# Two cross attentions on one core: their second halves with the chunk of heads as the outer loop and the block of keys as the inner one

## What is computed

```python
# layer 0: q and k are normalised per head; only keys with padding_mask count
attn = jnp.einsum('bihd,bjhd->bhij', q, k)
attn = jnp.where(padding_mask[:, None, None, :], attn, -jnp.inf)
ctx = jnp.einsum('bhij,bjhd->bihd', jax.nn.softmax(attn, axis=-1), v)
# layer 1: a mask per query and key
scores = jnp.einsum('bhqd,bhkd->bhqk', Q, K) / jnp.sqrt(jnp.float32(D))
scores = jnp.where(mask == 1, jnp.float32(-1000000000.0), scores)
out = jnp.einsum('bhqk,bhkd->bhqd', jax.nn.softmax(scores, axis=-1), V)
```

## Time and profile before

| | |
|---|---|
| median of 3 runs | 1674.43 us |
| lowest, highest | 1670.66, 1679.79 us |
| the profiled execution | 1673.19 us |
| its span in the trace | 1671.4 us |
| mean granted TensorE clock | 0.974 |
| L0x, second half | about 263 to 431 us |
| L1x, second half | about 1135 to 1321 us |

### The profile page before, as it was taken

One profiled execution on the slowest core, in us unless ns is written; L12 is line 12 of the kernel. 1 busy time (PEld: TensorE's weight loads), 2 busy tenths in 40 slices (PEclk: granted clock), 3 DMA queues, 4 the chain that ended last, 5 costly groups with the idle time before them and its releaser, 6 DMA issues. The chain is left out here.

```text
span 1671.4 us, 27782 instructions
## 1 busy us (share of the span) xinstructions
PE 1574.9 (94%) x9252; PEld 752.7 (45%) x9263; DVE 1025.3 (61%) x1708; ACT 523.2 (31%) x781; POOL 170.0 (10%) x126
## 2 busy tenths in 40 slices
PE   7999999999899889999999999998999899989997
PEld 3233332222333377666774433332222244477775
DVE  6778897999656541111112799998889746652223
ACT  3534555778213310000101111116567413200000
POOL 0522021000002010000002222102000001020002
PEclk9999998999999989999999999998999999989999
DMA  4433433220076667767762332113221021249996
GB/s 170 157 121 131 163 138 103 59 52 25 2 154 124 226 244 246 252 240 261 253 215 70 115 126 99 65 38 133 63 75 38 1 88 33 102 162 322 330 332 223
DMA packets 74460, 240.28 MB, mean 144 GB/s; under 512 B 7600, under 2 KB 21824, under 8 KB 55072
## 3 DMA queue, kind: packets, MB, share of 16 engines
q1 hardware_dynamic: 64752, 220.42, 39.6%
q10 hardware_dynamic: 7088, 10.69, 1.8%
q0 software_dynamic: 2560, 8.39, 1.5%
HBM read 214.04 MB, written 35.91 MB: 150 GB/s over the span
## 5 line engine op out<-in xcount | busy, mean ns | idle before, releaser
L1607 ACT ACTIVATE BIG<-banks 128x1024 f32<-128x1024 f32 (+5 forms) x320 | 282.2, 934 | 121.1 <-PE banks L1553 120.4
L1128 DVE CUSTOM_DVE_ANT_0 BIG<-banks,MASK,MX 128x512 bf16<-128x512 f32 (+5 forms) x384 | 229.1, 655 | 67.1 <-issue 38.7
L2173 PE MATMUL banks<-KF,BIG 128*128 128x160 f32 (+1 forms) x1792 | 229.0, 289 | 1.9 <-DVE KF L1870 1.9
L2173 PEld LDWEIGHTS banks<-KF,BIG 128*128 128x128 f32 x1792 | 226.9, 191 | 8.8 <-issue 8.8
L711 PE MATMUL banks<-KF,XN 32*128 32x512 f32 (+4 forms) x1280 | 188.4, 607 | 11.2 <-DVE MX L1128 3.3
L2143 PE MATMUL banks<-BIG,PB 128*128 128x512 f32 x448 | 198.0, 595 | 0.0
L1546 PE MATMUL banks<-XN,KF 32*128 32x512 f32 (+4 forms) x1280 | 187.8, 613 | 7.5 <-ACT BIG L1607 5.2
L1658 DVE TENSOR_TENSOR PB<-PB,BIG 128x2048 f32<-128x2048 f32 (+5 forms) x78 | 165.7, 2124 | 21.6 <-ACT BIG L1607 19.2
L1119 DVE TENSOR_REDUCE MXW<-banks 128x2 f32<-128x1024 f32 x128 | 149.4, 1216 | 29.0 <-PE banks L711 28.9
L1513 PE MATMUL banks<-BIG,V 128*32 128x512 f32 (+4 forms) x1280 | 159.8, 568 | 4.5 <-ACT BIG L1607 2.4
L2143 PEld LDWEIGHTS banks<-BIG,PB 128*128 128x128 f32 x448 | 82.9, 190 | 100.6 <-issue 100.5
(11 more groups left out here) (298 smaller groups left out, 1482.4 us busy)
## 6 DMA issues: line engine op xcount, KB each, us to landing
BIG<-in_L0f_w SPq DMA_DIRECT2D x64, 1024.0 KB, 4.8
BIG<-in_L1f_w SPq DMA_DIRECT2D x48, 1024.0 KB, 5.7
BIG<-in_mask_q SPq DMA_DIRECT2D x16, 1024.0 KB, 9.0
k_saved<-KF SPq DMA_DIRECT2D x32, 256.0 KB, 2.7
CT<-in_ctx SPq DMA_DIRECT2D x6, 1024.0 KB, 4.8
XNT<-in_ctx SPq DMA_DIRECT2D x6, 1024.0 KB, 5.6
v_saved<-V SPq DMA_DIRECT2D x24, 256.0 KB, 2.4
KF<-k_saved SPq DMA_DIRECT2D x24, 256.0 KB, 3.4
```

Source lines behind the costliest of these rows:

```text
L1128: last = v.tensor_tensor_reduce(m.JUNK[:, 2 * half + e, k0:k1], pair[:, e, k0:k1], bias, 1.0, mx, ALU.add, ALU.max, mx)
L1607: a.activation(m.PE_[:, s % NP, 2 * half:2 * half + 2, q0:q1], m.pair[(2 * s + half) % 3][:, :, q0:q1], ACT.Exp).then_inc(exp_ready, 1)
L2173: last = t.matmul(out, W1[k][:, d, f * P:(f + 1) * P], XE[:, d, :], start=d == 0, stop=d == DC - 1)
```

## The change

`weighted_by_chunk` takes the place of `weighted_values` in the two cross attentions (the self attentions keep the latter, without its dynamic parts). It loops over chunks outside and blocks inside. A **unit** is one chunk with one block, 4 steps. The first unit of a chunk uses the block in SBUF; the others (`others`) load a unit's keys, values and mask into a ring of 3 slots (KRING, VRING, and MBK or ROWRING). A chunk's products with V stay in one PSUM bank over all blocks and are copied out once (`copy_out`). The PSUM pairs begin anew with each chunk. Masks are made once, in the first half, saved with the keys and loaded with them: L1x has a new load, four new GpSimd instructions and a store of 512 KB per block there (`turned_mask`, `keep_mask`); L0x has one new VectorE instruction and a store of 128 KB (KEYROW). The clearing of PSUMS and OACC goes. The value for masked scores, NEG, is now -2^100.

```diff
+RING = 3
 # first half, sync
+            def keep_mask(j):
+                if L.row_mask:
+                    wait_alone(sp, masks_made, j * KT_ + KT_ + B)
+                    sp.dma_start(m.MSAVE[one(j)].rearrange("a p k n -> (a p) k n"), m.MBK[RING]).then_inc(mask_stored, 16)
+                else:
+                    wait_alone(sp, bias_ready, j + 1 + B)
+                    sp.dma_start(m.ROWSAVE[one(j)].rearrange("a p n -> (a p) n"), m.KEYROW).then_inc(mask_stored, 16)
...
 # first half, gpsimd
-            for c in range(DC):
-                g.memset(m.PSUMS[c], 0.0).then_inc(zeroed, 1)
-            g.memset(m.OACC[:, :, :], 0.0).then_inc(zeroed, 1)
...
+            def turned_mask(j):
+                pool.wait_ge(masks_loaded, j * 16 + 16 + B)
+                wait_alone(pool, mask_stored, j * 16 + 16 + B)
+                for kb in range(KT_):
+                    g.tensor_scalar(m.MBK[RING][:, kb, :], m.MK[:, kb, :], 1.0, m.RN[:, 0:1], ALU.is_equal, ALU.mult).then_inc(masks_made, 1)
...
 # first half, vector
+                v.tensor_scalar(m.KEYROW, m.KM[:, 0:KB], m.mask_factor, m.mask_offset, ALU.mult, ALU.add).then_inc(keys_counted, 1)
...
 # second half
+    GROUPS = -(-(NB - 1) // RING)
...
+    def others(eng, nb, c, body):
+        with eng.Fori(0, GROUPS) as group:
+            for r in range(RING):
+                with eng.If(group * RING + (r + 1) < nb):
+                    body(Unit(nb, c, group, r))
...
+            def load(u):
+                at, c, r = u.group * RING + u.r, u.c, u.r
+                wait_alone(sp, product_done, u.step(-KT_) + BP)
+                block = bass.ds(at, 1)
+                sp.dma_start(m.KRING[:, r, :], m.KSAVE[block, :, c, :].rearrange("a p n -> (a p) n")).then_inc(keys_loaded[r], 16)
...
+            for c in range(DC):
+                others(sp, nb, c, load)
+                if c == 0:
+                    O.load_output_weights(sp)
...
+            def unit(u):
+                flag = flag_of(u)
+                for k in range(1, KT_):
+                    scores(u, k, flag)
+                    times_values(u, k - 1)
...
+                with pe.If(at + 1 < nb):
+                    scores(follower, 0, flag_of(follower))
+                if u.c + 1 < DC:
+                    with pe.If(at + 1 >= nb):
+                        next_chunk(u.c)
+                times_values(u, KT_ - 1)
...
+            for c in range(DC):
+                unit(Unit(nb, c))
+                others(pe, nb, c, unit)
...
+            def copy_out(c):
+                dve.wait_ge(product_done, nb * (KT_ * c + KT_) + BP)
+                v.tensor_copy(m.OACC[:, c, :], m.bank[6 + c % 2]).then_inc(chunk_done, 1)
```

More of the change, by code:

```diff
@@ L1437, in weighted_values, with tile_free @@
     kt = L.order
[L1438 to L1446 removed]
+    m.fresh = []
+    O = project_out(nc, m, L, next_loaded, None)
+    def tile_free(s):
+        return max(0, s - NP + 1)
     class Parts:
@@ L1526, in scores @@
                     M.ready(pe, 1)
[L1527 to L1528 removed]
                 ks = slice(kt[k] * P, (kt[k] + 1) * P)
[L1530 to L1533 removed]
+                parts = BIAS_PARTS[L.fixed] if kt[k] in (0, KT_ - 1) else 1
                 def out(g):
@@ L1543, in scores @@
                 for g in range(G):
-                    if not biases and g % 2 == 0:
-                        pe.wait_ge(exp_ready, i * (2 * NS) + max(0, 2 * s - 2 + g // 2) + B)
-                    t.matmul(out(g), m.KF[rows(g), c, ks], m.QF[rows(g), c, q0:q1], start=not biases, stop=False)
-                if L.row_mask:
-                    with pe.If(flag > 0):
-                        for g in range(G):
-                            t.matmul(out(g), m.IDB[:, :], m.MBK[:, kt[k], q0:q1], start=False, stop=False)
@@ L1551, in scores @@
-                stationary = m.KEYROW[:, ks] if whole else m.ONEB[:, :]
+                    t.matmul(out(g), m.KF[rows(g), c, ks], m.QF[rows(g), c, q0:q1], start=False, stop=False)
                 for g in range(G):
-                    last = t.matmul(out(g), stationary[rows(g, NROW), :], m.SHIFT[rows(g, NROW), c, q0:q1], start=False, stop=True)
+                    last = t.matmul(out(g), m.ONEB[rows(g, 3), :], m.SHIFT[rows(g, 3), c, q0:q1], start=False, stop=True)
                     if g % 2:
@@ L1583, in gpsimd @@
+            for s in range(1, NS + 1):
+                if s < NS:
+                    scores(s)
+                times_values(s - 1)
+            O.tensor(pe, sum_taken, NS, added_up, DC)
         @staticmethod
@@ new lines, in vector @@
+            for s, (c, k) in enumerate(steps):
+                q0, q1 = L.queries_of[kt[k]]
+                if k == 0 and (q0, q1) != (0, T):
+                    v.memset(m.PSUMS[c], 0.0).then_inc(sum_zeroed, 1)
+                    dve.wait_ge(sum_zeroed, c + 1)
+                dve.wait_ge(exp_ready, s * 2 + 2)
+                dve.wait_ge(sum_taken, s)
+                dst = m.PSUMS[c][:, :, q0:q1]
+                if k == 0 and (q0, q1) == (0, T):
+                    v.tensor_copy(dst, m.PE_[:, s % NP]).then_inc(sum_taken, 1)
+                else:
+                    v.tensor_tensor(dst, dst, m.PE_[:, s % NP, :, q0:q1], ALU.add).then_inc(sum_taken, 1)
+                if k == 1 and c:
+                    add_up(c - 1)
```

399 lines of the change are left out of this document (232 added, 167 removed).

## The result

| | before | after |
|---|---|---|
| median | 1672.55 us | 1724.2 us |
| lowest, highest | 1668.88, 1679.79 us | 1720.48, 1734.59 us |
| the profiled execution, its span | 1673.19, 1671.4 us | 1726.84, 1725.1 us |
| mean granted TensorE clock | 0.974 | 0.963 |

The changed kernel is slower: the ratio of its time to the time of the kernel before is 1.0314 (95% interval 1.0285 to 1.0343). The forecast was 1738 us with a range of 1700 to 1785.

A forecast was written before the change was run, and what follows sets the result against it. TensorE, nearly full in the second halves, was taken to bound the kernel, VectorE's lag showing only at the end. Terms of -1.2, 29, 22, 10, 4 and 1 gave +65 us on 1673.2: 1738 us, range 1700 to 1785.

The forecast's parts named there:

- gaps at six changes: At the second halves' chunk changes, 16 idle jumps leave TensorE idle 4.4 us (L0x) or 5.2 us (L1x): +29 us.
- clock falls at the changes: After each of the six chunk changes TensorE's clock falls to about half, losing 3.7 us each: +22 us.
- exits: At each second half's end, idle jumps and half clock delay the denominators: +5 us each, +10 us.
- boundaries inside a chunk, L1x: At 12 unit boundaries in L1x's second half, two flag reads exceed the queued work, 0.3 us each: +4 us.
- starts: At the second halves' starts, TensorE waits less for the first mask row and copies: -1.2 us together.
- first halves: One more VectorE row per block in L0x, four more GpSimd instructions per block in L1x: +1 us.
- the rivals for the engine that decides: At chunk changes ScalarE and VectorE make the same 16 jumps and might return last; TensorE was assumed; no size or chance.
- The rival in which the clock stays at 2.4 GHz (1711 us): At chunk changes TensorE's clock stays up, without 22 us and 5 of 10 at the ends: 1711 us, chance 0.11.
- The faster rival (1666 us): At chunk ends, TensorE's queue hides jumps (under 0.14 us each); only lag and start wait go: 1666 us, chance 0.07.
- Missed code (1792 us): Jumps leave TensorE's fetched code, stalling 1.7 us at each jump back at chunk ends: 54 us more, 1792 us, chance 0.09.
- Late ring loads (1754 us): In L1x's second half, TensorE waits for keys in 8 units, 2 us each: 1754 us, chance 0.07.

The follow-up runs named there:

- one group on some engines: Two runs of the changed kernel, loop turning once instead of five times: on TensorE alone, 1675.9 us; on ScalarE, VectorE and SyncE alone, 1722.8 us.
- five groups: The changed kernel itself, whose loop over groups of blocks turns five times per chunk on every engine: 1724.2 us, ratio 1.0314 to the kernel before.
- three in L0x: The changed kernel with its loop over groups of blocks turning three times instead of five, as seen in L0x: 1687.7 us, ratio 1.0088.
- The run with small adds: The kernel before, with VectorE's 32 adds into OACC cut to one column of 512: 1670.2 us, ratio 0.9988.
- the one with one group: The changed kernel with its loop over groups of blocks turning once instead of five times on every engine: 1662.7 us, ratio 0.9945 to the kernel before.

## Why the prediction was right, step by step

The second halves account for the sum. L0x's took 21.9 us more and L1x's 28.9 us more, together 50.8 of the 53.7 us between the two profiled executions (1726.84 against 1673.19). Of the other 2.9 us, 0.9 stand ahead of L0x's start and 2.1 behind L1x's exit, most of them in one wait of 1.64 us for a DMA in the last mixture (0.27 before).

| term | forecast, us | measured, us |
|---|---|---|
| gaps at six changes | +29 | +28.6 |
| clock falls at the changes | +22 | +13.6 |
| exits | +10 | +9.0 (4.4 and 4.7) |
| boundaries inside a chunk, L1x | +4 | 0 |
| starts | -1.2 | -1.3 |
| first halves | +1 | +0.9 in L1x, none shown in L0x |

**Gaps: right.** Both parts held, 0.37 us a jump and 2.3 us of queued work that hides them. The gaps were forecast at 4.4 and 5.2 us and are 4.29 and 5.24 in the mean. Of the rivals for the engine that decides, which no row of before could settle, the runs with one group on some engines decided for TensorE.

**The clock: the mechanism right, the size off.** This is the term that was sized worst, 22 us for 13.6. I took the smaller of two losses at the starts of the halves, 3.7 us, for each fall. Measured are 1.5 to 2.9 us, 2.3 in the mean. At the starts the array came from several waits in a row and stayed at 1.2 GHz for 10 us and more (0.51 over 12 us in the earlier trace rows); behind one gap of 4 to 5 us it is at 0.57 to 0.81 over 8 to 10 us, and part of the low stretch may lie in the gap, where it costs nothing (0.80 from 442 to 448 us, almost all of it the gap ahead of the denominators). The lower bound that I gave, 1.6 us a fall, was nearer. The rival in which the clock stays at 2.4 GHz (1711 us) is refuted for five groups and true for three in L0x.

**Exits: right, for a reason half seen.** The prediction had 12.5 us from the last product's start to the denominators' end; 11.9 and 11.6 came. It set this against the lag of VectorE before. The run with small adds gives 6.5 without most of the lag, and the one with one group 4.5 without the lag and without the block loop's three idle turns. So of the 3.0 us between 7.5 and 4.5 the lag was the smaller part and the idle turns the larger.

**Boundaries: forecast 4, measured 0.** With one group the pitch in L1x is 43.5 us. Before, blocks there take 38.9 us, and 57.6 us for the one with mask products; (3 x 38.85 + 57.6) / 4 = 43.5. Two flag reads and their register steps at each unit's end are thus hidden in full, also in L1x.

**First halves: near 0.** L1x's, from its first block to the wait ahead of the second half, took 193.8 us against 192.9, and 191.3 with one group: without the late jump told above, the new masks cost nothing there. L0x's ended 2 us late in this one execution, with the granted clock at 0.66 from 206 to 216 us where it was 1.00 before. That says nothing of the new row: in the eleven profiled executions with this first half TensorE's last product ahead of the second half (L1306) starts between 260.3 and 267.8 us, against 261.1 and 260.4 in the two with the old one, and the late ones have the clock down in some earlier stretch. What the row costs stays unknown below that scatter; the earliest are no later than before.

**The faster rival (1666 us)** needed jumps under 0.14 us or none of them, and a loop without them ran in 1662.7 us. Its condition was not met, and its sum came near partly by luck: it put 6 us at the two exits down to VectorE's lag alone, where the run with small adds gives 1.5 us for it and the rest goes with the three idle turns. **Missed code (1792 us)** did not happen at the six changes, where the gap grows by the same 0.37 us for every jump. **Late ring loads (1754 us)** did not happen: in one group's run the pitch leaves no room for them.

## What to carry to other kernels

In this kernel a static loop whose turns are skipped by tests costs TensorE's queue 0.37 us for every test and jump back; put inside an outer loop it is paid each time, and whatever exceeds the 2.3 us of work queued ahead shows as idle time put down to issue. Before the nesting of two loops is exchanged, multiply the idle turns of the one that becomes the inner, and count the loop by a register if the program allows it. Take work off an engine only where a wait for it stands on the path: here 17 us less on VectorE bought about 1.5 us over two exits, and the three idle turns at each exit leave TensorE idle for 1.75 us.

## What was not expected of the hardware

- Behind a gap the loss to the clock didn't grow with the gap: 13.6 us for six gaps of 4.1 to 5.3 us and 12.8 us for six of 8.6 to 9.8 us. Gaps of 1.2 to 1.4 us lost nothing.
- ScalarE, with the same 16 skipped tests and jumps, came back 2.5 us after its last exponential, TensorE 5.2 us after its last products began: ScalarE's branches are recorded at 45 ns, TensorE's at 208.
- In all eight runs in which TensorE's loop over groups is more than a single fixed turn, TensorE was idle 0.9 to 2.2 us longer at one place in L1x's first half, far from the loop over groups, and in none of the five others. There a transfer of instructions starts 2.7 to 3.0 us ahead of the late jump, against 5.0 to 5.3 us in the others; that it is the cause is not shown.
